# A four-layer conditioned stack: values' products from split operands, the root behind gelu 1, the small network a block later

## The chip, the cores and the metric

One core of one Trainium2 chip. Five engines with queues of their own work beside each other: TensorE (PE; its weight loads are PEld), VectorE (DVE), ScalarE (ACT), GpSimd (POOL) and SyncE (SP), which here issues nearly all DMAs. SBUF is the memory on the chip, PSUM the banks (128 partitions of 512 floats) that TensorE writes. The metric is the device time of one launch in microseconds.

## The reference, cut to what matters

`x` is 64 sequences of 64 tokens of width 256, with one condition vector per sequence. Four layers follow each other: 0, attention with 16 heads of 64, and a gelu MLP of 1024; 1, attention with 16 heads of 16 and a gated MLP of 682; 2, attention with heads of 16, a gelu MLP of 1024 and a gelu-tanh gate (`x + (gelu(v) * tanh(g)) @ W`); 3, a low-rank layer whose matrices a small network makes from the condition. Norms in front of attentions and MLPs are scaled and shifted by the condition. What the change touches:

```python
h = _modulate(_layernorm(x), sh_msa, sc_msa)        # layer 0
q, k, v = jnp.split(h @ W_qkv, 3, axis=-1)          # 16 heads of 64 each
out = jnp.einsum('bhqk,bkhd->bqhd', softmax(q k), v)
y = (x - m) * rsqrt(v + eps)                        
h = gelu(_layernorm(ada_emb) @ W1 + b1); w = h @ W2 + b2   # layer 3's small network
```

## The kernel before, in words

`x` stays in SBUF, transposed (`X`, two halves of 128 features by 4096 tokens), and is worked through in `NCH` = 8 chunks of 512 tokens. The stages follow each other: attention 0, gelu MLP 0 (the first gelu stage), attention 1, gated MLP 1, attention 2, gelu MLP 2 (the second gelu stage), the gelu-tanh gate (the gate stage), the low-rank layer. In each stage an engine has its own hand-written order of instructions and waits on semaphores (`wait_ge`) for what others produce. Between stages stands a barrier.

Where precision must hold and speed too, a float32 operand is split into a high part (float32r, a rounded form) and the remainder; `split3` (L441 to L445) makes three products of float32r operands: low weights by high data, high by low, high by high. `Weights` (L168 to L221) loads raw pieces of 128x512 by groups on SP's queue (`load`), ScalarE copies the high parts (`high`, L196; it waits for a whole group's DMAs), VectorE or POOL subtract the low parts (`low`, L206), and `ready` is TensorE's wait for the first n pieces.

**Attention 0** (L495 on). A step is one pair of heads j of 8 in chunk c. TensorE's step: scores `S` of this pair, transposes of the previous pair's weights (`TRA`) and of the output before (`TRB`), projection of the next pair's Q and K (`pe_proj`, 12 products of 512 columns), the previous pair's output `O`, six output products by `WO`, and, in every second step, `pe_v` (L611): the values of the next two pairs of heads for all 512 tokens, into banks 0 and 1, half of the tokens each. Before, these are float32 products of `H32` and `WV`, 64 tokens as weights by 128 columns, in the two column halves of the array. ScalarE copies bank 0 out (`act_v`, L641), VectorE bank 1 (`dve_v`, L649); the next projection writes over both banks once they are copied. The norm of the next chunk is spread over the steps by constants (`M_NORM` the root and scaling, `M_HH` and `M_HL` the split of H, `M_D`, `M_SQ` and so on). `M_VAR` is step 1 of the next chunk, called tail, where TensorE makes the variance into bank `TRB` and VectorE reads it (`dve_v` of `Front`, L369).

**The start.** SP loads x chunk 0, half of the modulation weights, weight group 0 (four 256 KB pieces of WQK), the other half, chunk 1, `WV` (1 MB), group 1, chunk 2, and later the rest. ScalarE and VectorE split pieces between the first norms.

**Gelu stage** (`feed_forward`, n_m = 8 blocks of 128 hidden features a chunk). TensorE runs the up products three blocks ahead of the down products into four banks. ScalarE writes gelu twice from each bank (`Gf` and the high part `Gh`), VectorE the low part (L1205), then the down products of the block may run. ScalarE waits with gelu m for the split of block m - 2. For the next chunk's norm ScalarE has at block 0 `act_rstd` (L289 to L294: table of ln and exp, the two functions; the gelu table comes back with the next gelu) and VectorE at block 1 Newton's three steps and the scaling (L374 to L382). At a chunk's end VectorE does the variance, the split of the next chunk's block 0 and the residual (L454), POOL adds it to X (L465, `X<-X,RT`).

**Gate stage** (four blocks a chunk; POOL idle). Up products of two matrices (12 products a block) two banks deep, gelu and tanh on ScalarE, on VectorE the product (L1194), high (L1203) and low part (L1205), six down products. Into it the small network of layer 3 is laid (`Hyper`, L1825): ten slots s. TensorE's step of a slot (`tensor`), ScalarE's (`scalar`: copies out or gelu) and VectorE's (`vector`) stood all in the same block: slot 2c in block 1 of chunk c, slot 2c + 1 in block 3, each behind the engine's own work of that block. Slot 0 has a layer norm of the condition in ten small VectorE steps with a root on ScalarE between them.

```python
for m in range(n_m):                      # ScalarE in the gate stage, cut
    act.wait_ge(a_ps.h, a_ps.at(g + 1))   # up products of block m
    nc.scalar.activation(Gf[m % 2][:], src, ACT.Gelu, bias=bias(0, m)).then_inc(g_act.h, 1)
    nc.scalar.activation(Gt[m % 2][:], BK[2 + m % 2][:], ACT.Tanh, bias=bias(1, m)).then_inc(g_act.h, 1)
    hyper.scalar(act, c, m)               # waits for TensorE's step of the slot
```

Of the kernel before, what the change touches and what calls it, by code (L numbers as in the profile page):

```python
# [13 lines left out]
P = 128  # L14
# [10 lines left out]
DH0 = 64  # L25
# [26 lines left out]
def cond_stack_kernel(nc, io):  # L52
    ctx = ExitStack()
    with ctx:
# [61 lines left out]
        c_set, c_sil, c_ang, c_sin, wv_in = count("c_set"), count("c_sil"), count("c_ang"), count("c_sin"), count("wv_in")  # L116
# [119 lines left out]
        class Front:  # L236
# [134 lines left out]
            def dve_norm(self, dve, c):  # L371

# [5 lines left out]
                nc.vector.scalar_tensor_tensor(out=V1[:], in0=V1[:], scalar=1.5, in1=V2[:], op0=ALU.add, op1=ALU.mult).then_inc(f_n3.h, 1)  # L378
                dve.wait_ge(f_n3.h, self.at(f_n3, c + 1))
# [100 lines left out]
        def attention0_plan():  # L480
# [4 lines left out]
            st.WV = place("WV0", [P, DH, 2, PAIRS, DH0], R + 49152)  # L485
# [4 lines left out]
                       for n in ns for k in range(DH)] for ns in ((0, 2), (1, 3))]  # L490
            groups += [[(wo[:, 2 * g:2 * g + 2], WO[0][:, 2 * g:2 * g + 2], WO[1][:, 2 * g:2 * g + 2], WOf[:, 2 * g:2 * g + 2]) for g in range(4)]]
            st.weights = Weights(groups, by_dve=range(8))
            return st

        def attention0(st, nxt):  # L495
            if True:
# [8 lines left out]
                work = Region(R + 57344, END)  # L505
# [105 lines left out]
                def pe_v(pe, G, jj, c, p):  # L611

                    for hf in range(2):
# [20 lines left out]

                def act_v(act, jj, c):
                    if jj % 2 == 0:
# [4 lines left out]
                        nc.scalar.activation(VP[(jj // 2) % 2][:, 0:4], BK[0][:].rearrange("p (b r d) -> p b r d", b=4, r=2), ACT.Copy).then_inc(va_sb.h, 1)  # L641

                def dve_v(dve, jj, c):
                    if jj % 2 == 0:
# [4 lines left out]
                        nc.vector.tensor_copy(VP[(jj // 2) % 2][:, 4:8], BK[1][:].rearrange("p (b r d) -> p b r d", b=4, r=2)).then_inc(vd_sb.h, 1)  # L649


                M_NORM, M_HH, M_HL = 2, 4, 5
# [17 lines left out]
                with nc.Block() as block:  # L670
                    @block.sync
                    def _(sp):
# [5 lines left out]
                        sp.dma_start(WV[:], io["l0_wv"].rearrange("(k p) (a r d) -> p k a r d", p=P, a=2, r=PAIRS)).then_inc(wv_in.h, 16)  # L678
# [14 lines left out]
                    def _(pe):  # L693
# [20 lines left out]
                        pe.wait_ge(wv_in.h, wv_in.at(16))  # L714
# [6 lines left out]
                        def step(c, j, p, more, tail=False, first=False):  # L721
# [65 lines left out]
                            if (not tail and (more or j < PAIRS - 1)) or (tail and more):  # L787
                                if jn % 2 == 0:
                                    pe_v(pe, g + 1, jn, cn, pn)
                            if not first and j == M_MEAN:  # L790
# [11 lines left out]
                        st.weights.ready(pe, st.weights.all())  # L802
# [72 lines left out]
                    def _(dve):  # L875
# [47 lines left out]
                        def step(c, j, p, more, tail=False, first=False):  # L923
# [29 lines left out]
                            if ahead:  # L953
                                dve_v(dve, jn, cn)
# [870 lines left out]
        class Hyper:  # L1825
# [112 lines left out]
            def vector(self, dve, c, m):  # L1938
                s = self.slot(c, m)
                if s is None:  # L1940
                    return
# [257 lines left out]
```

## Time and profile before

| | us |
|---|---|
| median of 3 runs | 2127.19 (2124.84 to 2128.36) |
| the profiled execution | 2128.56 |
| its span, first to last instruction | 2126.8 |
| TensorE busy | 1911.8 |
| VectorE, ScalarE, POOL busy | 1319.5, 994.4, 787.6 |
| mean granted clock of TensorE | 0.96 |

A row of a group of instructions reads: line, engine, operation, output<-inputs, count | busy us, mean ns of one | idle before it and the releaser. A row in order of time: start, length (of the merged run of instructions), engine, line, operation; in brackets what the engine idled before it and for whom. The granted clock is a share of 2.4 GHz: 1.00, or 0.50 for 1.2 GHz. The length of a TensorE record holds its way through the array; how close products follow each other is told by their starts.

### The profile page before, as it was taken

To read this page: it belongs to the slowest core of one execution; us is meant where nothing else is said; L and a number is where in the kernel's file an instruction comes from. 1 tells how busy PE (TensorE), PEld (TensorE's weight loads), DVE (VectorE), ACT (ScalarE), POOL (GpSimd) and SP (SyncE) were. 2 spreads that over 40 slices of the span, in tenths; PEclk is the share of its full clock that TensorE was granted. 3 is DMA by queue.
4 is the path that set the end of the run, shared out by engine and by line. 5 is a ranking of instruction groups with operands and counts; after the bars stand their busy time and mean duration, and the time that the engine had idled before them with its cause. 6 is when DMAs were issued, how large, how long until landed. Compare 5 with 4: busy or idle time off the path is not lost. (4 is left out here: it accounts for less than half of the span.)

```text
span 2126.8 us, 44677 instructions
## 1 busy us (share of the span) xinstructions
PE 1911.8 (90%) x17318; PEld 1485.0 (70%) x17318; DVE 1319.5 (62%) x2028; ACT 994.4 (47%) x1693; POOL 787.6 (37%) x737
## 2 busy tenths in 40 slices
PE   5999999999979998688988899969999799988898
PEld 4777777777867776466766777747777677766675
DVE  4454555555554555588898577768888555544455
ACT  3433433443336666365666344324555466643222
POOL 1220211121123334566677333456878533340000
PEclk8999999999999999799999999979999899999999
DMA  5100000000010000100000000010000000003222
GB/s 184 70 2 2 2 2 2 2 2 2 2 41 21 0 0 1 45 2 3 2 2 2 27 0 0 0 41 2 2 0 2 27 5 0 0 21 103 75 70 80
DMA packets 26300, 44.73 MB, mean 21 GB/s; under 512 B 4240, under 2 KB 12240, under 8 KB 26000
## 3 DMA queue, kind: packets, MB, share of 16 engines
q1 hardware_dynamic: 24848, 42.01, 6.0%
q8 instruction: 132, 2.16, 0.4%
q10 hardware_dynamic: 1280, 0.23, 0.1%
q14 instruction: 40, 0.33, 0.0%
HBM read 35.94 MB, written 6.29 MB: 20 GB/s over the span
## 5 line engine op out<-in xcount | busy, mean ns | idle before, releaser
L1205 DVE TENSOR_TENSOR Glb<-Gfb,Ghb 128x512 fp32r<-128x512 f32 x176 | 165.2, 948 | 97.6 <-ACT Ghb L1156 95.9
L443 PE MATMUL bank<-HH,W1b 128*128 128x512 f32 x448 | 184.9, 413 | 16.1 <-PEq L1511 7.1
L325 POOL TENSOR_TENSOR Tm<-Dv,MOD 128x512 f32<-128x512 f32 x94 | 108.4, 1173 | 236.9 <-DVE Dv L382 159.1
L444 PE MATMUL bank<-HL,W1b 128*128 128x512 f32 x448 | 177.3, 396 | 0.0
L445 PE MATMUL bank<-HH,W1b 128*128 128x512 f32 x448 | 177.2, 396 | 0.0
L443 PE MATMUL O<-Ghb,W2b 128*128 128x512 f32 x352 | 142.9, 406 | 37.1 <-DVE Glb L1205 37.0
L463 POOL TENSOR_TENSOR spare<-RT 128x1 f32<-128x1 f32 x32 | 6.4, 201 | 401.1 <-DVE RT L454 401.1
L314 POOL TENSOR_TENSOR XS<-Tm 128x512 f32<-128x512 f32 x48 | 69.8, 1454 | 219.1 <-ACT Tm L280 214.2
L445 PE MATMUL O<-Ghb,W2b 128*128 128x512 f32 x352 | 138.0, 392 | 0.0
L444 PE MATMUL O<-Glb,W2b 128*128 128x512 f32 x352 | 137.8, 391 | 0.0
L1386 PE MATMUL bank<-WQKa,HH 128*128 128x512 f32 x256 | 91.6, 441 | 38.8 <-DVE HL L390 16.6
L622 PE MATMUL bank<-WV,H 128*64 128x128 f32 x2048 | 120.5, 276 | 2.0 <-ACT Q L631 2.0
L622 PEld LDWEIGHTS bank<-WV,H 128*64 128x64 f32 x2048 | 112.8, 138 | 13.5 <-issue 13.4
L443 PEld LDWEIGHTS bank<-HH,W1b 128*128 128x128 f32 x448 | 85.9, 192 | 41.7 <-issue 17.9
L1662 ACT ACTIVATE PTa<-bank 128x512 f32<-128x512 f32 x128 | 69.2, 593 | 97.6 <-PE bank L1542 97.6
L649 DVE COPY VP<-bank 128x512 f32<-128x512 f32 x32 | 22.1, 691 | 147.9 <-PE bank L622 147.9
L443 PEld LDWEIGHTS O<-Ghb,W2b 128*128 128x128 f32 x352 | 66.3, 188 | 67.9 <-DVE Glb L1205 55.3
L443 PE MATMUL bank<-HH,WQK 128*128 128x512 f32 x256 | 107.5, 420 | 4.3 <-DVE HL L390 4.3
L1155 ACT ACTIVATE Gfb<-bank,bias_cols 128x512 f32<-128x512 f32 x128 | 87.8, 686 | 45.9 <-PE bank L445 37.4
L838 ACT ACTIVATE PT<-bank 128x512 f32<-128x512 f32 x64 | 38.3, 598 | 149.1 <-PE bank L743 148.9
L332 POOL TENSOR_TENSOR H<-Tm,MOD 128x512 f32<-128x512 f32 x94 | 98.5, 1069 | 11.8 <-POOL Tm L325 10.6
L444 PE MATMUL bank<-HL,WQK 128*128 128x512 f32 x256 | 101.6, 397 | 0.0
(262 smaller groups left out, 5161.6 us busy)
## 6 DMA issues: line engine op xcount, KB each, us to landing
w<-l_w_dram SPq DMA_DIRECT2D x33, 256.0 KB, 3.4
X<-xT_dram SPq DMA_DIRECT2D x16, 256.0 KB, 6.7
out_dram<-XO SPq DMA_DIRECT2D x8, 512.0 KB, 2.7
wm<-w_mods_dram SPq DMA_DIRECT2D x4, 768.0 KB, 5.1
W2b_f<-l_w_dram SPq DMA_DIRECT2D x11, 256.0 KB, 5.5
WQK_f<-l_wqk_dram SPq DMA_DIRECT2D x8, 256.0 KB, 8.6
W1b_0f<-l_w_dram SPq DMA_DIRECT2D x8, 256.0 KB, 3.7
wm<-w_mods_dram SPq DMA_DIRECT2D x4, 384.0 KB, 6.3
```

What stands on the lines that cost most here:

```text
L314: nc.gpsimd.tensor_tensor(XS[:], Tm[:, 0], Tm[:, 1], ALU.add).then_inc(f_ss.h, 1)
L325: nc.gpsimd.tensor_tensor(Tm[:, k].rearrange("p (b t) -> p b t", t=T), Dv[:, k].rearrange("p (b t) -> p b t", t=T), m, ALU.mult).then_inc( ...
L332: last = nc.gpsimd.tensor_tensor(H32[p][:, k].rearrange("p (b t) -> p b t", t=T), Tm[:, k].rearrange("p (b t) -> p b t", t=T), m, ALU.add)
L443: nc.tensor.matmul(out, w_lo_ap, x_hi, start=first, stop=False)
L444: nc.tensor.matmul(out, w_hi_ap, x_lo, start=False, stop=False)
L445: return nc.tensor.matmul(out, w_hi_ap, x_hi, start=False, stop=last)
L622: last = nc.tensor.matmul(BK[hf][h2 * T:(h2 + 1) * T, b * P:(b + 1) * P], H32[p][:, k, bb * T:(bb + 1) * T], WV[:, k, h2, jj:jj + 2, :], s ...
L838: nc.scalar.activation(PT[(j + 1) % 2][:].rearrange("p t q -> p (t q)"), TRA[:], ACT.Copy).then_inc(pt_sb.h, 1)
L1155: nc.scalar.activation(Gf[m % 2][:], src, ACT.Gelu, bias=bias(0, m))
L1205: nc.vector.tensor_tensor(Gl[m % gb][:], gf, Gh[m % gb][:].bitcast(F32), ALU.subtract).then_inc(g_lo.h, 1)
L1386: last = nc.tensor.matmul(QKB[:], (HH, HL)[xp][p][:, k, t * P:(t + 1) * P], WQK[wp][:, k], start=(i == 0 and k == 0), stop=(i == 2 and k = ...
L1662: nc.scalar.activation(PT[:, 4 * i:4 * i + 4].rearrange("p r q -> p (r q)"), bank[:], ACT.Copy).then_inc(pt_sb.h, 1)
```

## The change

In attention 0 the values are made from the split H (`HH`, `HL`) and a split `WV`: for each half of the tokens two blocks of 128 tokens, two halves of the features and three products of 256 columns (both heads groups side by side), 24 a call. Since the values now lie 128 tokens deep, each copy to `VP` becomes four of 64 partitions by 256. `WV` is split like the other weights, in pieces 4 to 7 of group 0, loaded with it; `WO` is split a step later, and TensorE waits for it at its first use. `M_HL` moves from 5 to 6; variance and its reader go ahead of the values' work in the tail step. In the gelu stages ScalarE's root moves from block 0 to block 1. In the gate stage TensorE's slots move to blocks 2 and 0 (of the next chunk), ScalarE's and VectorE's parts to blocks 3 and 2; the layer norm and its root stay in block 1 of chunk 0.

```diff
@@ class Front @@
             def dve_norm(self, dve, c):
+                self.dve_newton(dve, c)
+                self.dve_scale(dve, c)
...
@@ attention0_plan @@
-            st.WV = place("WV0", [P, DH, 2, PAIRS, DH0], R + 49152)
+            WV = st.WV = [place(f"WV0_{i}", [P, DH, 2, PAIRS * DH0], R + 49152 + 8192 * i, F32R) for i in range(2)]
+            WVf = place("WV0_f", [P, DH, 2, PAIRS * DH0], R + 49152 + 8192)
+            wv = io["l0_wv"].rearrange("(k p) (a n) -> k p a n", p=P, a=2)
...
+            groups[0] += [(wv[k][:, a], WV[0][:, k, a], WV[1][:, k, a], WVf[:, k, a]) for k in range(DH) for a in range(2)]
...
-            st.weights = Weights(groups, by_dve=range(8))
+            st.weights = Weights(groups, by_dve=range(12))
@@ attention0, pe_v @@
-                        for b in range(CB // 2):
+                        for i in range(2):
+                            tok_ = slice((2 * hf + i) * P, (2 * hf + i + 1) * P)
+                            out = BK[hf][:, i * 2 * P:(i + 1) * 2 * P].rearrange("p (a n) -> p a n", a=2)
                             for k in range(DH):
-                                for h2 in range(2):
-                                    bb = hf * CB // 2 + b
-                                    last = nc.tensor.matmul(BK[hf][h2 * T:(h2 + 1) * T, b * P:(b + 1) * P],
-                                                            H32[p][:, k, bb * T:(bb + 1) * T], WV[:, k, h2, jj:jj + 2, :],
-                                                            start=(k == 0), stop=(k == DH - 1), skip_group_check=True)
+                                for xp, wp in ((0, 1), (1, 0), (0, 0)):
+                                    last = nc.tensor.matmul(out, (HH, HL)[xp][p][:, k, tok_], WV[wp][:, k, :, jj * DH0:(jj + 2) * DH0],
+                                                            start=(k == 0 and wp == 1), stop=(k == DH - 1 and xp == 0 and wp == 0))
                         last.then_inc(v_ps.h, 1)
@@ act_v (dve_v alike, with tensor_copy and the second bank) @@
-                        nc.scalar.activation(VP[(jj // 2) % 2][:, 0:4], BK[0][:].rearrange("p (b r d) -> p b r d", b=4, r=2), ACT.Copy).then_inc(va_sb.h, 1)
+                        for a, b in ((0, 0), (1, 0), (0, 1), (1, 1)):
+                            last = nc.scalar.activation(v_dst(jj, 0, a, b), v_src(0, a, b), ACT.Copy)
+                        last.then_inc(va_sb.h, 1)
...
-                M_NORM, M_HH, M_HL = 2, 4, 5
+                M_NORM, M_HH, M_HL = 2, 4, 6
@@ sync @@
-                        sp.dma_start(WV[:], io["l0_wv"].rearrange("(k p) (a r d) -> p k a r d", p=P, a=2, r=PAIRS)).then_inc(wv_in.h, 16)
@@ tensor @@
-                        pe.wait_ge(wv_in.h, wv_in.at(16))
+                        st.weights.ready(pe, 8)
                         pe_v(pe, 0, 0, 0, 0)
...
                                 if jo == 0:
+                                    st.weights.ready(pe, st.weights.all())
                                     pe.wait_ge(out_taken.h, out_taken.at(2 * c))
...
                             if (not tail and (more or j < PAIRS - 1)) or (tail and more):
+                                if tail and j == M_VAR:
+                                    f, cc = early(fr, nf, c - 1, more)
+                                    f.pe_var(pe, cc)
                                 if jn % 2 == 0:
                                     pe_v(pe, g + 1, jn, cn, pn)
...
-                            if tail and j == M_VAR:
-                                f, cc = early(fr, nf, c - 1, more)
-                                f.pe_var(pe, cc)
...
-                        st.weights.ready(pe, st.weights.all())
@@ scalar @@
                         step(0, 1, 0, 2, first=True)
+                        st.weights.high(act, 4)
@@ vector @@
+                            if tail and j == M_VAR:
+                                f, cc = early(fr, nf, c - 1, more)
+                                f.dve_v(dve, cc)
                             if ahead:
                                 dve_v(dve, jn, cn)
...
-                            if tail and j == M_VAR:
-                                f, cc = early(fr, nf, c - 1, more)
-                                f.dve_v(dve, cc)
...
+                        st.weights.low(dve, 4)
                         step(0, 1, 0, 2, first=True)
@@ feed_forward @@
-                M_NORM, M_HH, M_HL = (1, 4, 4) if n_m == 8 else (1, 3, 3)
+                M_RSTD, M_NEWTON, M_NORM, M_HH, M_HL = (1, 1, 1, 4, 4) if n_m == 8 else (0, 1, 1, 3, 3)
...
-                                if f and f.norm and m == 0:
+                                if f and f.norm and m == M_RSTD:
                                     f.act_rstd(act, cc)
...
+                                if f and f.norm and m == M_NEWTON:
+                                    f.dve_newton(dve, cc)
                                 if f and f.norm and m == M_NORM:
-                                    f.dve_norm(dve, cc)
+                                    f.dve_scale(dve, cc)
@@ class Hyper @@
-                s = 2 * c + {1: 0, 3: 1}.get(m, -99)
+                s = 2 * c + {2: 0, 0: -1}.get(m, -99)
+                return s if s >= 0 else None
+
+            def after(self, c, m):
+
+                s = 2 * c + {3: 0, 2: -1}.get(m, -99)
                 return s if s >= 0 else None
...
             def scalar(self, act, c, m):
-                s = self.slot(c, m)
+                if (c, m) == (0, 1):
+                    act.wait_ge(l3_ln.h, l3_ln.at(6))
+                    nc.scalar.activation(self.st[:, 3:4], self.st[:, 2:3], ACT.Sqrt).then_inc(l3_act.h, 1)
+                s = self.after(c, m)

```

## Rows read from the trace of the kernel before

**Rows 1.** The page of the kernel before: busy time of each engine.
```profile
PE 1911.8 (90%) x17318; PEld 1485.0 (70%) x17318; DVE 1319.5 (62%) x2028; ACT 994.4 (47%) x1693; POOL 787.6 (37%) x737
```

**Rows 2.** Stretches: a chunk, the gate stage. Length; busy PE, PEld, DVE, ACT, POOL; clock; DMA.
```profile
83.60:153.90 70.30, 69.08 (x981) 55.96 (x981) 37.57 (x62) 28.85 (x51) 11.88 (x11) 1.00 0.01 2
...
1907.60:2088.90 181.30, 162.68 (x666) 121.76 (x666) 83.79 (x140) 52.28 (x81) 0.00 (x0) 0.93 0.25 78
```

**Rows 3.** TensorE's waits in the gate stage, then in the first gelu stage.
```profile
PE O L443 <- DVE Glc L1205: 18.5, 6, 4.9
...
PE O L443 <- DVE Glb L1205: 18.2, 19, 1.8
```

**Rows 4.** TensorE in order of time (start us, us): a values' call, the next.
```profile
190.32 3.71 PE L622 MATMUL bank<-WV,H 128*64 128x128 f32 x64
193.96 0.69 PE L734 MATMUL S<-KT,Q 64*64 64x64 f32 x32
```

**Rows 5.** TensorE in order of time: wide split products; a later attention's output products.
```profile
196.21 0.39 PE L443 MATMUL bank<-HH,WQK 128*128 128x512 f32 x1
196.44 0.40 PE L444 MATMUL bank<-HL,WQK 128*128 128x512 f32 x1
...
1500.70 1.16 PE L1577 MATMUL O<-OSa,WOa 128*128 128x128 f32 x8
```

**Rows 6.** Copies and their nearest row (groups, one line's view); engines behind a call.
```profile
L649 DVE COPY VP<-bank 128x512 f32<-128x512 f32 x32 | 22.1, 691 | 147.9 <-PE bank L622 147.9
...
L1430 DVE TENSOR_TENSOR VBa<-bank,VBIa x64: 405/422/429, 1405.1 to 1670.5; 64x256 f32<-64x256 f32 x64
...
197.02 0.64 DVE L942 TENSOR_TENSOR OL<-bank,OH 128x512 fp32r<-128x512 f32 x1
...
198.98 0.50 PE L443 MATMUL O<-OH,WO 128*128 128x512 f32 x1
```

**Rows 7.** The start: one stretch as in rows 2, then engines in order.
```profile
8.20:20.20 12.00, 6.18 (x28) 4.11 (x28) 5.86 (x17) 3.13 (x4) 1.26 (x1) 1.00 0.90 301
...
20.25 2.17 ACT L196 ACTIVATE WQK<-WQK_f 128x512 fp32r<-128x512 f32 x4
...
40.21 3.09 DVE L206 TENSOR_TENSOR WQK<-WQK_f,WQK 128x512 fp32r<-128x512 f32 x4 [3.77 <-ACT WQK L196]
...
42.29 5.38 PE L622 MATMUL bank<-WV,H 128*64 128x128 f32 x64 [2.04 <-ACT Q L631]
```

**Rows 8.** A gelu stage, VectorE, POOL and TensorE in order of time.
```profile
723.63 0.68 DVE L1205 TENSOR_TENSOR Glb<-Gfb,Ghb 128x512 fp32r<-128x512 f32 x1
...
726.25 2.39 POOL L465 TENSOR_TENSOR X<-X,RT 128x1024 f32 x1
...
727.66 1.53 DVE L1205 TENSOR_TENSOR Glb<-Gfb,Ghb 128x512 fp32r<-128x512 f32 x1 [1.63 <-ACT Ghb L1156]
...
729.24 0.50 PE L443 MATMUL O<-Ghb,W2b 128*128 128x512 f32 x1 [0.79 <-DVE Glb L1205]
...
733.16 0.50 PE L443 MATMUL O<-Ghb,W2b 128*128 128x512 f32 x1 [0.91 <-DVE Glb L1205]
```

**Rows 9.** The gate stage: engines in order of time, then stretches as in rows 2.
```profile
1921.28 0.20 ACT L1923 ACTIVATE st<-st 64x1 f32<-64x1 f32 x1 [2.60 <-DVE st L1956]
...
1924.82 1.28 ACT L1158 ACT_TABLE_LOAD   x1
...
1948.95 1.94 PE L1905 MATMUL S<-w,hT 128*64 128x512 f32 x8
...
1954.65 0.79 PE L443 MATMUL O<-Ghc,W2c 128*128 128x512 f32 x1 [3.77 <-DVE Glc L1205]
...
1954.60:1957.40 2.80, 2.75 (x7) 2.17 (x8) 1.72 (x3) 0.00 (x0) 0.00 (x0) 0.50 0.21 80
2052.50:2068.80 16.30, 16.30 (x74) 13.49 (x73) 9.60 (x15) 6.00 (x10) 0.00 (x0) 1.00 0.16 57
1977.60:2004.00 26.40, 23.21 (x97) 16.27 (x96) 11.79 (x19) 8.93 (x15) 0.00 (x0) 0.94 0.25 80
```

More of the change, by code:

```diff
@@ L115, in cond_stack_kernel @@
         x_in = [count(f"x_in{i}") for i in range(3)]
-        c_set, c_sil, c_ang, c_sin, wv_in = count("c_set"), count("c_sil"), count("c_ang"), count("c_sin"), count("wv_in")
+        c_set, c_sil, c_ang, c_sin = count("c_set"), count("c_sil"), count("c_ang"), count("c_sin")
         pos_in, h_lead, ct_in = count("pos_in"), count("h_lead"), count("ct_in")
@@ L371, in dve_norm, with dve_newton @@
             def dve_norm(self, dve, c):
+                self.dve_newton(dve, c)
+                self.dve_scale(dve, c)
+            def dve_newton(self, dve, c):
                 dve.wait_ge(f_rs.h, self.at(f_rs, c + 1))
@@ L504, in attention0 @@
                 nf.live_in(TRB[:], TRB[:], lambda f, pe, c: None, lambda f, pe, c: None, lambda e, c: h_free(e, c + NCH), False, x_final)
-                work = Region(R + 57344, END)
+                work = Region(R + 65536, END)
                 Q = [work.take(f"Q0_{i}", [P, CH]) for i in range(2)]
@@ L633, in act_proj, with v_src, v_dst @@
                     nc.scalar.activation(KT[jj % 2][:], BK[1][:], ACT.Copy).then_inc(ka_sb.h, 1)
+                def v_src(hf, a, b):
+                    return BK[hf][b * T:(b + 1) * T, :].rearrange("p (i a n) -> p i a n", i=2, a=2)[:, :, a]
+                def v_dst(jj, hf, a, b):
+                    return VP[(jj // 2) % 2][a * T:(a + 1) * T].rearrange("p (f i b) r d -> p f i b (r d)", f=2, i=2)[:, hf, :, b]
                 def act_v(act, jj, c):
@@ L648, in dve_v @@
                             dve.wait_ge(o_ps.h, o_ps.at(2 * gr - 2))
-                        nc.vector.tensor_copy(VP[(jj // 2) % 2][:, 4:8], BK[1][:].rearrange("p (b r d) -> p b r d", b=4, r=2)).then_inc(vd_sb.h, 1)
-                M_NORM, M_HH, M_HL = 2, 4, 5
+                        for a, b in ((0, 0), (1, 0), (0, 1), (1, 1)):
+                            last = nc.vector.tensor_copy(v_dst(jj, 1, a, b), v_src(1, a, b))
+                        last.then_inc(vd_sb.h, 1)
+                M_NORM, M_HH, M_HL = 2, 4, 6
                 M_XH, M_MEAN, M_D, M_SQ, M_SQH = 3, 4, 5, 5, 6
@@ L787, in step @@
                             if (not tail and (more or j < PAIRS - 1)) or (tail and more):
+                                if tail and j == M_VAR:
+                                    f, cc = early(fr, nf, c - 1, more)
+                                    f.pe_var(pe, cc)
                                 if jn % 2 == 0:
                                     pe_v(pe, g + 1, jn, cn, pn)
+                            elif tail and j == M_VAR:
+                                f, cc = early(fr, nf, c - 1, more)
+                                f.pe_var(pe, cc)
                             if not first and j == M_MEAN:
@@ L952, in step @@
                                                         ALU.mult).then_inc(o_sb.h, 1)
+                            if tail and j == M_VAR:
+                                f, cc = early(fr, nf, c - 1, more)
+                                f.dve_v(dve, cc)
                             if ahead:
@@ L1938, in vector @@
             def vector(self, dve, c, m):
-                s = self.slot(c, m)
-                if s is None:
-                    return
                 st, ada, ada2, gB = self.st, self.ada, self.ada2, self.gB
-                if s == 0:
+                if (c, m) == (0, 1):
                     dve.wait_ge(l3_in.h, l3_in.at(112))
@@ L1961, in vector @@
                     step(nc.vector.tensor_copy(st[:, 5:6], st[:, 4:5]))
+                s = self.after(c, m)
+                if s is None:
+                    return
                 if s >= 3 and s - 3 < 4:
```

3 lines of the change are left out of this document (1 added, 2 removed).

## The prediction, made before the change was run

> **What bounds the kernel now.** The page comes first: TensorE is busy 90% of the span and no other engine passes 62%, so time is won by taking work off TensorE or by ending its waits [rows 1]. Then the busy time of two stretches [rows 2]. In a steady chunk of the first attention TensorE is busy 69.08 of 70.30 us at the full clock: there its own work is the time, eight such chunks long. The gate stage is busy 162.68 of 181.30 us at a mean clock of 0.93. Last the waits of TensorE: in the gate stage 18.5 us in six waits, all for a split on VectorE; in the first gelu stage 18.2 us in 19 waits for the same line, two in each of its 8 chunks and three more at its end [rows 3]; the second has two in each of 7 chunks. So each part of the change is judged against TensorE: the products directly, the two moved steps by those waits.
>
> **1. The values' products.** Before, one call (a pair of heads' pairs, 32 in all) issues 32 products that show as 64 records: it starts at 190.32 and the next work at 193.96, 3.64 us [rows 4]. After, it issues 24 products of 256 columns against 128 weights. No row shows a product of that kind and width. From above: the same kind with 512 columns starts every 0.228 us (196.21, 196.44, and so on through the 12 of a projection [rows 5]). 24 of those would be 5.47 us, slower than before; that end is the rival below. From below: 512 columns at 2.4 GHz are 0.213 us, so 256 can't go under 0.107, 2.57 us a call. The nearest row in weights and stream is the output product of the later attentions: eight records, each loading 128 weights, take 1.16 us with the last one's 0.275 in it, so 0.126 apart [rows 5]. The 512-column product lies 0.015 over its columns; 0.107 + 0.015 = 0.122 agrees. I take 0.122: 2.93 us a call, 0.71 saved, times 32 = 22.7 us. With 0.112 it would be 30, with 0.133 still 14.
> The loading of weights needs a word. The Trainium skill (TensorE: Matmul & The Clock Gate, Part 3, The mechanism) says that a weight load overlaps a running matmul only where their row groups differ. By that rule every new product, which uses all rows, would pay its load on top, some 0.107 us by the page's weight-load formula: 0.21 each, 5.1 us a call, 47 us lost over the calls. The trace speaks against it: the eight records above have 0.126 between them for load and stream together.
>
> Evictions. VectorE's copy of 128x512 (0.691 us) becomes four of 64x256; the nearest row, 64x256 from PSUM, is 0.422 [rows 6]. Four are 1.7 us, 1 us more per call, and I take the same for ScalarE. ScalarE does its half while TensorE still works on the second. VectorE begins at the call's end; behind its copy it has the maximum, the subtraction, the sum and OL, which starts at 197.02 for a TensorE product at 198.98 [rows 6]: finished 1.3 us early, 0.3 to 0.4 early after the change. Covered, narrowly; were it not, each tenth late costs 3 us over 32 calls. HL moves from a step with a call to one without, and has the time of the products and the next scores. The variance products go ahead of the call in the tail step, and their reader on VectorE ahead of its copies, so the longer copies don't delay the transposes that reuse that bank. Cost zero.
>
> The start. The 1 MB of values' weights is now in the first group, ahead of the second half of the modulation weights and of chunk 1, on SP's one queue. ScalarE's first `high` waits for the whole group, at 20.25. Then 0.5 + 0.8 + 2.1 MB must have landed; the queues moved 301 GB/s from 8.2 to 20.2, 3.6 MB [rows 7]. Just in time. The half behind it (0.8 MB, 2.6 us more at that rate) can be half a microsecond late for TensorE, which later waits for HL anyway. The first call will wait for VectorE's four `low`, 40.21 + 3.09 = 43.3, where it now starts at 42.29 [rows 7]: 1 us. The split of WO is now a step later: four copies on ScalarE, then four on POOL, each pass no shorter than VectorE's 3.09, and the first output products come a step on, some 9 us. 0 to 1 us. I book 1 us in all: **-22 us** for the stage.
>
> **2. The gelu stages.** Now ScalarE does the root (table, logarithm, exponential, table back) ahead of gelu 1; after, behind it. Follow one chunk [rows 8]. Gelu 1 comes behind the root and the load of its table, its split starts at 727.66 and lasts 1.53 us, and TensorE starts at 729.24 after a wait of 0.79. Then VectorE does Newton's three steps, the scaling and the split of block 2, and TensorE goes on at 733.16 after 0.91. After the change gelu 1 is done before the root, its split follows the residual (which ends as POOL begins, 726.2), and the first wait is gone. The second need not be. The split of 1.53 us shows why: VectorE, reading two operands of SBUF, stood still until POOL's X+RT (726.25 to 728.64) ended; by itself such a split is 0.68 (723.63) [rows 8]. Newton's first step, now at about 726.6, gets in ahead of X+RT or waits for it; the second waits in any case until near 729.4 and ends at 730.1. Third step 0.7 (a split's length), scaling 1.2 (twice as wide), split 0.7: TensorE starts block 2 at 732.7 to 733.0 where it was 733.16. The removed wait comes back at the next block. I take 0.35 us for each of the 15 chunks with both waits (8 and 7): **-5 us** (0 to 7; were POOL no obstacle, all of 2 us a chunk, 28 us).
>
> **3. The gate stage.** ScalarE, in block 1 and in block 3, waits for the small network's step that TensorE does behind its own block; only then come the next gelu and tanh and VectorE's three steps. In block 3 two blocks of up products cover that; in block 1 nothing does: the network's step starts at 1948.95 and takes 1.94; then ScalarE copies and does gelu and tanh, VectorE its three steps, and TensorE goes on at 1954.65, 3.77 us idle [rows 9]. After, TensorE's steps stand in blocks 2 and 0, their readers in blocks 3 and 2. The reader in block 3 comes when gelu and tanh of that block are long done, and the next two up products and a down product (4.1 us at least) lie before the first result that it delays; the reader in block 2 finds the step done and has two down products and a up product for cover. Of the 18.5 us in six waits the first has 4.9, one at the stage's end 0.6 (it stays); the other four go, 13.0 in all. The first shrinks: the root of the layer norm stays in block 1, but the copy behind TensorE's transpose no longer sits ahead of the table back. That load stands at 1924.82; behind the root (1921.28, 0.20) it could stand at 1921.5 [rows 9], so TensorE goes on 3.3 us earlier and 1.6 to 1.9 us remain. After such a wait the clock is at 1.2 GHz: 2.80 us at 0.50 [rows 9], in which six products take 2.73 us and not 1.36. Four of these go, 5.6 us, and half of the first one's 2. Sum 13.0 + 3.3 + 5.6 + 1.0, and 0.7 for the pipeline's refill: 23.6. Check: a chunk with the network takes 26.4 us, one without 16.3 at full clock [rows 9]; two steps of 1.94 with their transposes explain about 4.8, so 5.3 a chunk is loss, 21 over four, plus the first one's 4. **-24 us** (-17 to -27). Past SP nothing moves; its weight loads and the writes of the network's results come half a block or more later, and the results are wanted only in the stage that follows, 30 us on.
>
> **Sum.** 22 + 24 + 5 = 51 us off the profiled execution's 2128.56: 2077.6. It stands 1.4 above the median 2127.19, so the forecast for the median is 2076.5.
>
> **The rivals.** (a) The narrow product costs what the wide one does, 0.228: each call takes 5.47 us, 1.83 more than now, +58 over 32 calls; with the -29 of the rest, 2157, slower. It decides from 0.152 a product upward in the stage, from 0.19 in the kernel. For it: no row shows this kind under 512 columns. Against: the 0.126 of rows 5. 5%. (b) The network's waits only change place: some reader or a bank of the pair holds TensorE up in another block. Half of part 3 stays, 2089. For it, ScalarE still waits at each step; against, the cover counted above. 10%. (c) VectorE's four copies come late: with 0.3 to 0.6 us late at 32 calls, 10 to 19 us return, 2087 to 2096. 9%. (d) POOL is in Newton's way less than I say: another 20 us, 2056. Against: the 1.53. 6%. (e) That the change does nothing: excluded by the count, 1024 products become 768 of another kind; the question is their price.
>
> **How the numbers follow.** My case has 70%, with 2062 (0.112 a product, 27 and 7 for the others) to 2098 (0.133, 17 and 0). The range 2060 to 2099 also takes in (b) and (c); outside lie (a), (d) and some of my own spread, under 2 in 10. A measurement tells 0.2%, 4 us, from no change. Faster 0.93, same 0.02, slower 0.05.
>
> **What would show it.** In the profile after: a call of 24 products 2.8 to 3.1 us long and chunks of 67.4 us; no wait of TensorE over 0.4 us behind the four copies; in the gelu stages one wait a chunk, of about 1.5 us, and Newton's second step stretched to over 2 us beside X+RT; in the gate stage one wait near 1.8 us, chunks of 21 us, and a clock at 1.00 from the second chunk on. I am wrong if the call is above 3.4 us, if gate chunks stay above 24 us, or if a gelu chunk is under 25.3 us (now 26.3).

## The result, and the profile after

The changed kernel takes 2075.15 us (median of 4 runs, 2071.4 to 2077.6), the kernel before 2127.65 in runs beside it (2124.8 to 2128.4): ratio 0.975, with an interval of 0.974 to 0.977. The forecast was 2076.5 in a range of 2060 to 2099. The profiled execution has a span of 2073.4 us where the one before had 2126.8, so 53.4 us went; the forecast's sum was 51.

Stage by stage, from TensorE's records. A stage is counted from the end of the last product of the stage before (the first one from the span's start) to the end of its own last product:

| stage | before | after | gone | forecast |
|---|---|---|---|---|
| first attention | 632.3 | 613.3 | 19.0 | 22 |
| first gelu stage | 222.9 | 217.6 | 5.3 | } 5 |
| second gelu stage | 210.6 | 205.8 | 4.8 | } |
| gate stage | 185.7 | 161.6 | 24.1 | 24 |
| all others | 875.4 | 875.1 | 0.3 | 0 |

The page of the changed kernel: TensorE's line, against [rows 1], and the groups of the values' products and VectorE's copies, against [rows 4, 6].
```profile
PE 1872.6 (90%) x16038; PEld 1464.3 (71%) x16038; DVE 1380.5 (67%) x2128; ACT 1028.9 (50%) x1793; POOL 799.0 (39%) x737
...
L669 DVE COPY VP<-bank 64x256 f32<-64x256 f32 x128 | 54.0, 422 | 114.0 <-PE bank L632 112.7
...
L632 PE MATMUL bank<-WV,HH 128*128 128x256 f32 x512 | 98.7, 286 | 2.7 <-DVE WV L206 2.7
```
TensorE has 39 us less work and is still busy 90% of the span, so its waits fell too. VectorE has 61 us more: 32 are the copies, 27 are Newton's second step (L380), which has the same 48 instructions as before and takes 62.2 us where it took 35.1. The copy costs the 422 ns that the nearest row said. The 286 ns of a product hold its way through the array; its price is the distance between starts.

A call of 24 products starts at 294.77 and the next work, at 297.74, is 2.97 us later. Its first products, TensorE in order of time:
```profile
294.77 0.28 PE L632 MATMUL bank<-WV,HH 128*128 128x256 f32 x1
294.88 0.28 PE L632 MATMUL bank<-WV,HL 128*128 128x256 f32 x1
295.01 0.41 PE L632 MATMUL bank<-WV,HH 128*128 128x256 f32 x2
295.25 0.28 PE L632 MATMUL bank<-WV,HL 128*128 128x256 f32 x1
```
2.97 over 24 is 0.124 apiece. Next the stretches (columns as in [rows 2]): two chunks of the first attention, a chunk of the first gelu stage, a gate chunk with the small network and one without.
```profile
291.65:428.38 136.73, 131.61 (x1641) 108.39 (x1640) 84.99 (x147) 65.47 (x124) 23.45 (x21) 1.00 0.01 2
...
727.56:753.39 25.83, 24.33 (x104) 19.07 (x103) 16.18 (x18) 16.38 (x24) 11.16 (x8) 1.00 0.00 0
...
1929.11:1950.39 21.28, 21.28 (x99) 15.11 (x100) 11.97 (x20) 7.22 (x11) 0.00 (x0) 1.00 0.29 99
...
2003.90:2020.20 16.30, 16.30 (x74) 13.49 (x73) 9.60 (x15) 5.99 (x9) 0.00 (x0) 1.00 0.25 85
```
In the gate stage TensorE is busy without a break at the full clock, where the chunk of 26.4 us had 0.94 [rows 9]. The gelu chunk still lacks 1.5 us, the attention's two lack 5.1. The waits that remain say where: the gate stage's two, the gelu stage's, then two groups of the first attention.
```profile
PE O L449 <- DVE Glc L1230: 2.7, 2, 2.2
...
PE O L449 <- DVE Glb L1230: 15.3, 10, 1.8
...
PE O L449 <- DVE OL L966: 7.8, 10, 2.5
PE S L795 <- DVE SP L955: 6.6, 14, 1.3
```
In the gate stage 18.5 us in six waits became 2.7 in two [rows 3]. In the gelu stage 19 waits became 10, but 18.2 us only 15.3: half of the waits went, the others grew. In the first attention TensorE now waits 6.6 us for SP, the scores' subtraction, where the same wait came to 1.8 us before. Behind it stands a second kind of wait (an output product, 3.6 us in six, most of them 0.63) that was not there before. The prediction had ruled out any wait over 0.4 us behind the copies.

### The profile page after: what moved, and what is told of

The parts are those of the page before. It is cut to its first block and busy times, and to the rows that moved or that the text cites. A ratio compares the mean times of both kernels' runs of the same rounds, so it can differ in the third digit from the quotient of the medians.

```text
span 2073.4 us, 42326 instructions
## 1 busy us (share of the span) xinstructions
PE 1872.6 (90%) x16038; PEld 1464.3 (71%) x16038; DVE 1380.5 (67%) x2128; ACT 1028.9 (50%) x1793; POOL 799.0 (39%) x737
## 5 line engine op out<-in xcount | busy, mean ns | idle before, releaser
L1230 DVE TENSOR_TENSOR Glb<-Gfb,Ghb 128x512 fp32r<-128x512 f32 x176 | 155.7, 894 | 67.0 <-ACT Ghb L1181 65.3
L469 POOL TENSOR_TENSOR spare<-RT 128x1 f32<-128x1 f32 x32 | 11.4, 355 | 397.9 <-DVE RT L460 397.9
L669 DVE COPY VP<-bank 64x256 f32<-64x256 f32 x128 | 54.0, 422 | 114.0 <-PE bank L632 112.7
L449 PE MATMUL bank<-HH,WQK 128*128 128x512 f32 x256 | 107.4, 420 | 4.6 <-DVE HL L396 4.6
L451 PE MATMUL bank<-HH,WQK 128*128 128x512 f32 x256 | 101.4, 396 | 0.0
L632 PE MATMUL bank<-WV,HH 128*128 128x256 f32 x512 | 98.7, 286 | 2.7 <-DVE WV L206 2.7
L450 PEld LDWEIGHTS bank<-HL,W1b 128*128 128x128 f32 x448 | 86.0, 192 | 20.8 <-issue 3.3
```

The lines of the kernel that those rows point to most:

```text
L449: nc.tensor.matmul(out, w_lo_ap, x_hi, start=first, stop=False)
L450: nc.tensor.matmul(out, w_hi_ap, x_lo, start=False, stop=False)
L451: return nc.tensor.matmul(out, w_hi_ap, x_hi, start=False, stop=last)
L632: last = nc.tensor.matmul(out, (HH, HL)[xp][p][:, k, tok_], WV[wp][:, k, :, jj * DH0:(jj + 2) * DH0], start=(k == 0 and wp == 1), stop=(k ...
L669: last = nc.vector.tensor_copy(v_dst(jj, 1, a, b), v_src(1, a, b))
L1230: nc.vector.tensor_tensor(Gl[m % gb][:], gf, Gh[m % gb][:].bitcast(F32), ALU.subtract).then_inc(g_lo.h, 1)
```

## The experiments

Ten kernels ran, the last two five times each and the others once. Beside them the kernel before took 2123.4 to 2125.1 us, 2.5 to 4.3 us less than beside the changed kernel, so single times are read only to that accuracy and the stage lengths carry the argument. Their own spread can be read from the stages whose code a run leaves alone. The gelu stages repeat within 0.3 us, with one trace 1.2 us shorter. The gate stage, changed, lies between 160.0 and 162.5 us. The first attention, in the six traces with the changed kernel's code there, lies between 611.4 and 615.6: differences of under 4 us in that stage say nothing.

**One part undone: the gate stage.** The network's step on TensorE and its readers on ScalarE and VectorE go back to blocks 1 and 3.
```diff
- s = 2 * c + {2: 0, 0: -1}.get(m, -99)
+ s = 2 * c + {1: 0, 3: 1}.get(m, -99)
- s = 2 * c + {3: 0, 2: -1}.get(m, -99)
+ s = 2 * c + {1: 0, 3: 1}.get(m, -99)
```


> The changed kernel, with the small network's steps back in blocks 1 and 3 on all three engines. My theory: the gate stage grows by 24 us, from about 157 to 181, with five waits of TensorE of 2.6 to 5 us and stretches at half clock behind them; all other stages stay within 1 us; 2099 us. The rival (the gate stage became shorter through something else, such as the stages ahead of it ending with a warmer clock): it grows by under 15 us.

2099.36 us; the gate stage 187.7 us long, 26 longer than changed. Every wait of before is back, to the tenth [rows 3]:
```profile
PE O L449 <- DVE Glc L1230: 18.5, 6, 4.9
```
So the gate part is worth what the forecast gave it (24.1 by the table above, 26.1 here), and it doesn't depend on the others.

**Another undone: the root in block 0.** `M_RSTD, M_NEWTON, M_NORM, M_HH, M_HL` go from (1, 1, 1, 4, 4) to (0, 1, 1, 4, 4).

> The changed kernel, with ScalarE's root of the gelu stages back in block 0. My theory: a gelu chunk goes from 25.8 back to 26.3 us and has two waits of 0.8 and 0.9 in place of one of 1.5; both gelu stages together lose 7 to 10 us; 2084 us. The rival (the other parts shortened the gelu stages, through the state in which they begin): the two stages stay within 2 us of the changed kernel's.

2089.36 us; the gelu stages 222.8 and 210.5, 5.2 and 4.7 longer. The chunk is 26.3 us again with waits of 0.78 and 0.88. The part is worth 10 us, not 5.

**What holds Newton's step: POOL's pass cut to one token.** In the gelu stages POOL adds RT to X for the first token of a chunk alone; the rest of the residual is left out.
```diff
+ t, r = (bass.ds(c * CH, 1), slice(0, 1)) if one else (tok(c), slice(0, CH))
- nc.gpsimd.tensor_tensor(X[:, :, tok(c)], X[:, :, tok(c)], RT[:], ALU.add)
+ nc.gpsimd.tensor_tensor(X[:, :, t], X[:, :, t], RT[:, :, r], ALU.add)
```


> The changed kernel, but in the gelu stages POOL adds one token of a chunk's residual to X and not all 512 (it leaves out the rest of that sum). My theory, that POOL's long sum keeps VectorE out of Newton's steps: the wait of 1.5 us in block 2 goes nearly whole, a gelu chunk takes 24.2 to 24.6 us, 2075 falls by 18 to 24. The rival, that the wait is VectorE's own chain of split, Newton, scaling and split: the chunk stays above 25.5 us and the time within 5 us.

2042.91 us; gelu stages 204.3 and 194.8, together 24 less than changed. TensorE's row of the first one falls from ten waits to three, all in the last chunk:
```profile
PE O L449 <- DVE Glb L1231: 4.2, 3, 1.5
```
The whole fell by 32, not 24: the gate stage lost 3.8, the second attention 2.5 and the swiglu stage 2.3 as well. A shorter pass at a stage's end may be the reason (see the last run); no run tests that by itself.

The changed kernel shows the same thing from the other side. VectorE and POOL in order of time:
```profile
730.47 0.69 DVE L378 SCALAR_TENSOR_TENSOR V<-V,V 128x512 f32<-128x512 f32 x1
731.19 2.77 DVE L380 TENSOR_TENSOR V<-V,V 128x512 f32<-128x512 f32 x1
734.00 0.69 DVE L382 SCALAR_TENSOR_TENSOR V<-V,V 128x512 f32<-128x512 f32 x1
...
730.56 2.85 POOL L471 TENSOR_TENSOR X<-X,RT 128x1024 f32 x1
```
Newton's second step, 0.69 when left alone, takes 2.77 and ends 0.55 after POOL's pass ends (733.96 against 733.41). The Trainium skill (SBUF — State Buffer, SBUF: two separate sides) says that POOL and a VectorE operation with two inputs in SBUF share one pair of ports by an exclusive lock, and the one that comes second waits for the whole instruction. This trace and this run agree, with 2.77 and 0.69.

**VectorE's residual ahead of its copies.** In the tail step VectorE took the four copies first, then the residual of the chunk before, then the scores' maximum. Now the residual comes first, before the variance's reader.
```diff
 if tail and j == M_VAR:
+    residual(c - 1)
     f, cc = early(fr, nf, c - 1, more)
     f.dve_v(dve, cc)
```


> The changed kernel, but in the first attention VectorE takes the residual of a finished chunk ahead of the variance and of the four copies in step 1, while TensorE makes the values, and not behind them. My theory, that the stage's new waits at a chunk's start (0.47 and 0.63 in step 2) come from copies and residual standing one behind the other: both go, a chunk takes 67.3 to 67.6 us in place of 68.4, the stage is 7 to 9 us shorter, 2067. The rival, that the copies alone (1.7 us) make VectorE late: the waits stay and the chunk is above 68.1.

2065.43 us; the first attention 606.5 us, 6.8 less (7 to 9 were expected). The two later kernels with this order have 606.1 and 605.4, so all three lie at least 4.9 us below the six traces without it. Here is what it cures, in the changed kernel, VectorE and then TensorE in order of time:
```profile
279.69 1.73 DVE L669 COPY VP<-bank 64x256 f32<-64x256 f32 x4 [2.27 <-PE bank L632]
281.45 1.41 DVE L460 SCALAR_TENSOR_TENSOR RT<-O,bias_cols,MOD 128x512 f32<-128x512 f32 x2
282.78 0.68 DVE L952 TENSOR_REDUCE mx<-S 128x8 f32<-128x512 f32 x1
283.49 0.69 DVE L955 TENSOR_TENSOR SP<-S,mx 128x512 f32<-128x512 f32 x1
...
284.44 0.69 PE L795 MATMUL S<-VP,PT 64*64 64x64 f32 x32 [0.47 <-DVE SP L955]
285.76 0.49 PE L449 MATMUL O<-OH,WO 128*128 128x512 f32 x1 [0.63 <-issue]
```
VectorE stood idle 2.27 us ahead of the copies, waiting for the call. The residual fits in there. Behind the copies it makes SP late, and then OL (284.93 to 285.57; the profile names no releaser for the second wait, but OL ends 0.19 us ahead of that product): 0.47 and 0.63 us of TensorE. The pair stands in five of the seven steps of this kind, 5.2 us together; in two, right behind the loop's pause (see below), it is missing. With the order changed all five pairs are gone, and a steady chunk takes 66.8 us (426.28 to 493.06) where it took 68.0. A pair of 1.25 and 0.63 early in the first chunk stays: it has another cause, told under the start.

**Newton's steps a block later.** (1, 1, 1, 4, 4) becomes (1, 2, 2, 4, 4), so that they miss POOL's pass.

> The changed kernel, but in the gelu stages VectorE does Newton's steps and the scaling behind the split of block 2 and not ahead of it; POOL's sum is whole. The same instructions in another order. My theory: split 2 has to wait for POOL's X+RT once (to about 0.5 us behind its end) and is then there before TensorE wants block 2, so the wait of 1.5 us goes; scaling ends at the same time as now, so H comes no later, but TensorE comes 1.7 us earlier to the next chunk's first up product, which wants HL, and 0.5 to 1 us of it may be lost there. A chunk of 24.2 to 25.2 us, 10 to 24 us off the total, 2052 to 2066. The rival, that Newton's steps are on a chain of their own through POOL and HL that sets the chunk: it stays at 25.6 us or more.

2085.49 us; the gelu stages 221.8 and 210.7, 4.2 and 4.9 longer. My expectation missed and the other one held. The wait moved from block 2 to block 4, VectorE and TensorE in order of time:
```profile
694.83 1.22 DVE L364 TENSOR_TENSOR Dv<-X,S 128x1024 f32<-128x1024 f32 x1 [4.52 <-POOL H L332]
695.97 0.69 DVE L1230 TENSOR_TENSOR Glb<-Gfb,Ghb 128x512 fp32r<-128x512 f32 x1
...
696.71 0.50 PE L449 MATMUL O<-Ghb,W2b 128*128 128x512 f32 x1 [1.50 <-DVE Glb L1230]
```
The centring (L364) waits for POOL's H, and the split that TensorE wants stands behind it. A steady chunk is 25.9 us, no better, and the last chunks have longer waits, up to 3.9 us. From the start of POOL's pass, the scaling now starts 5.04 us later where it was 4.16, and H ends 11.15 us later where it was 10.73, while TensorE, without the wait in block 2, comes 1.5 us sooner to block 4. Of the two ways tried in this stage, taking POOL's pass away wins and going round it does not.

**Products of half the width.** Each product of 256 columns is made as two of 128, so a call has 48.
```diff
+for a in range(2):
...
-last = nc.tensor.matmul(out, (HH, HL)[xp][p][:, k, tok_], WV[wp][:, k, :, jj * DH0:(jj + 2) * DH0],
+last = nc.tensor.matmul(out[:, a], (HH, HL)[xp][p][:, k, tok_], WV[wp][:, k, a, jj * DH0:(jj + 2) * DH0],
```


> The changed kernel, but each values' product of 256 columns is made as two of 128 columns, with the same weights loaded for both: 48 products a call, the same columns in sum. What sets the price of a product? If the columns alone do, with 0.015 us over them, a product takes 0.068, the call 3.3 us, and the first attention grows by 10 us. If the load of 128 weights does (0.107 to 0.126 in the nearest rows), it is 0.11 to 0.13, the call 5.2 to 6 us, and the stage grows by 70 to 100 us. If this kind of product costs four times as much under 256 columns, 0.22 a product, the call is 10.6 us and the stage grows by 240 us. I expect the second.

2167.65 us, the first attention 92 longer. Three products take 0.336 us, TensorE in order of time:
```profile
300.00 0.28 PE L633 MATMUL bank<-WV,HL 128*128 128x128 f32 x1
300.11 0.39 PE L633 MATMUL bank<-WV,HH 128*128 128x128 f32 x2
300.33 0.27 PE L633 MATMUL bank<-WV,HL 128*128 128x128 f32 x1
```
So 0.112 us for half of the columns, where 256 columns take 0.124: a product of this kind has a floor of about 0.11 us. 48 by 0.112 is 5.4 us a call, 2.4 more than changed, 77 of the 92 us over 32 calls. Of the other 15, 4.6 are idle time where the loop goes round: four pauses, 8.8 us in all, where the changed kernel has two of 4.2. Over the 7.4 and 7.2 us from the first pause of each pair on, the granted clock is 0.54, which loses 5 us more than in the changed kernel; the rest isn't followed. As expected, the second case held. This run shows a floor, not its cause. That it is the load of a product's 128 weights, which every product has whatever its width, is the likeliest reading; no run tests it.

**HL left where it was.** `M_HL` back from 6 to 5, a step with a call.

> The changed kernel, with the split of H (HL) back in step 5 of the first attention, a step with a values' call, right behind VectorE's four copies. My theory: the copies end 1 us later than before, HL (1.2 to 1.6 us) pushes maximum, subtraction and OL out, and TensorE waits 0.7 to 1.3 us once a chunk before the output product or OL: the stage grows by 5 to 10 us. The rival, that HL is covered in both places: within 2 us.

2090.48 us; the first attention 14.2 us longer, above the 5 to 10 that I expected; the rival (within 2 us) fell. The wait for SP grows from 6.6 us in 14 times to:
```profile
PE S L795 <- DVE SP L955: 14.4, 23, 1.2
...
252.26 1.73 DVE L669 COPY VP<-bank 64x256 f32<-64x256 f32 x4 [3.82 <-PE bank L632]
254.02 1.88 DVE L396 TENSOR_TENSOR HL<-H,HH 128x1024 fp32r<-128x1024 f32 x1
```
There VectorE has HL behind the four copies, in the same step. SP then keeps TensorE waiting 1.06 us in each chunk, and OL, right behind, 0.58 us (the waits for OL grow from 7.8 us in ten to 12.9 in 19). With that order the narrow products would have won 5 us, not 19. The move of HL is what pays out the products.

**POOL's pass a chunk later.** POOL stood idle from 747.66 to 755.87 in the changed kernel's chunk. Its X+RT of a chunk goes there, near the end of the next chunk, in the gelu and swiglu stages.
```diff
-residual_pool(pool, c)
+if c > 0:
+    residual_pool(pool, c - 1)
+if not more:
+    residual_pool(pool, c)
...
-chunks(pool, body)
+chunks(pool, body, True)
```


> The changed kernel with one step of POOL moved: in the gelu and swiglu stages the sum X+RT of a chunk is no longer done right behind the chunk's residual, beside Newton's steps, but near the end of the next chunk, where POOL stood idle from 747.7 to 755.9 and VectorE has nothing but splits. The whole computation is done. Theory (POOL's pass holds VectorE's Newton step, and that is all of the wait of 1.5 us): as with the pass cut to one token, the wait goes and the gelu stages lose 20 to 26 us together, chunk 24.2 us, kernel 2049 to 2055 us. Rival 1 (the gain of the small pass came because POOL had less work in all, or because X was written with less traffic): the gelu stages stay within 5 us of the changed kernel's 217.6 and 205.8. Rival 2 (the pass now holds the splits of blocks 6 and 7 and the wait only changes place): a new wait of TensorE of 0.5 to 1 us a chunk for a split, 8 to 12 us gained.

2058.67 us, 4 above the 2049 to 2055 expected; gelu stages 204.7 and 195.6, together 23 less, as expected. One stretch and the rows of VectorE and POOL show the chunk without a wait, and Newton's step at its own length:
```profile
700.37:724.41 24.04, 24.04 (x104) 19.16 (x103) 15.91 (x19) 17.57 (x24) 10.88 (x8) 1.00 0.00 0
...
704.00 0.69 DVE L380 TENSOR_TENSOR V<-V,V 128x512 f32<-128x512 f32 x1
...
719.11 2.52 DVE L1230 TENSOR_TENSOR Glb<-Gfb,Ghb 128x512 fp32r<-128x512 f32 x1 [0.43 <-ACT Ghb L1181]
...
718.68 2.40 POOL L471 TENSOR_TENSOR X<-X,RT 128x1024 f32<-128x1024 f32 x1
```
The pass now holds a split instead (2.52 us and not 0.68), but that one is early, and TensorE doesn't notice. Some is given back: the second attention takes 2.7 us more and the swiglu stage 4.0. In the last chunk the pass stood behind the fills of the next stage's buffers, and VectorE's last residual waited for it:
```profile
825.36 1.41 DVE L460 SCALAR_TENSOR_TENSOR RT<-O,bias_cols,MOD 128x512 f32<-128x512 f32 x2 [5.77 <-POOL X L471]
```

**Both orders together.** The last one and the residual ahead of the copies.

> Both orders that the runs point to: POOL's X+RT of the gelu and swiglu stages a chunk later, and in the first attention VectorE's residual ahead of the variance's reader and of the four copies of the tail step. The whole computation is done. They touch different stages, so the gains should add: 20 to 26 us in the gelu stages and 6.8 us in the first attention (as measured alone), 2042 to 2049 us against 2075.2 of the changed kernel and 2127.7 of the one before: ratio to the latter 0.960 to 0.963. If the gelu part gives nothing, 2068, ratio 0.972.

2050.55 us median of 5 (2046.8 to 2052.8), ratio to the kernel before 0.965, interval 0.964 to 0.967; slower than the 2042 to 2049 expected, which had left out what the later pass gives back. First attention 606.1 (7.2 less than changed), gelu stages 203.5 and 195.6 (24.3 less), second attention 5.0 more, swiglu 2.0 more.

**The pass ahead of the fills.**

> As the kernel with both orders, but in a stage's last chunk POOL's X+RT of the chunk before comes ahead of the fills of the next stage's buffers and not behind them. In the kernel with both orders it stood behind 8 us of fills, VectorE's last residual waited 5.8 us for it and the second attention began with 9.6 us without a product where the changed kernel had 5.5. Theory: these 4 us come back at the second attention, and up to 2 at the swiglu stage's end: 2044 to 2047 us against 2050.6, ratio to the kernel before 0.962 to 0.964. Rival (the stage waits for the fills themselves, now 2.5 us later): nothing is gained, 2050 to 2053.

2048.45 us median of 5 (2044.5 to 2052.5), ratio 0.965, interval 0.963 to 0.966: not to be told apart from the last. The median lies between what I expected (2044 to 2047) and the rival (2050 to 2053). TensorE's gap at the second attention's start is 8.6 us, 1 less than the 9.6 of the last two kernels and well over the changed kernel's 5.5; the stage takes 317.7 us, where the two kernels with the same later pass took 318.7 and 321.0. POOL and ScalarE at that point, first in this kernel:
```profile
806.54 2.03 POOL L1349 MEMSET VBa<- 128x544 f32 x4
...
814.66 2.34 POOL L471 TENSOR_TENSOR X<-X,RT 128x1024 f32<-128x1024 f32 x1
...
817.32 1.28 ACT L1664 ACT_TABLE_LOAD   x1 [12.25 <-PEq L1112]
```
and in the changed one:
```profile
825.33 2.02 POOL L1345 MEMSET VBa<- 128x544 f32 x4
...
833.50 2.34 POOL L471 TENSOR_TENSOR X<-X,RT 128x1024 f32<-128x1024 f32 x1
...
836.16 1.28 ACT L1660 ACT_TABLE_LOAD   x1 [8.87 <-PEq L1111]
```
In both the next stage begins 0.3 us after POOL's last pass ends. POOL's fills and passes are what the stage's end waits for, and a pass put among them lengthens it, ahead of the fills or behind them. Of the 4 us that were to come back, the gap shows 1, so the rival is the nearer of the two.

## Why the prediction was right

**The price of a product** was the disputed number: 0.122 us taken, 0.124 measured, so 0.67 us a call and 21.4 over 32 calls instead of 22.7. Of the rivals, (a) put it at 0.228 and fell. The other rule it weighed, that the weights' load comes on top (0.21), fell as well: 0.124 and, at half the width, 0.112, both of products that use all rows. Some luck is in how well it fits. The forecast added 0.015 us to the time of the columns; at 128 columns that would be 0.068, and the run of half width has 0.112. And the row of 0.126 that seemed to agree is of float32 products, two records each; float32r products of that width stand 0.112 apart.

**The copies, "Covered, narrowly"**, at a cost of zero, are the step that failed. It counted the copies, the maximum, the subtraction, the sum and OL behind a call, and left out that in the tail step the residual's 1.41 us stand in that queue too. There the slack was used up, and TensorE waited up to 0.47 and 0.63 us where the forecast had "no wait of TensorE over 0.4 us": 5.2 us in five steps. Moving the residual alone gave 6.8 us back, so rival (c) was real, at 5 to 7 us and five calls, not 10 to 19 at 32.

**The move of HL** was also booked at nothing. Its sign is right and its size hidden: left where it was, HL would have cost 14.2 us.

**The start** was booked at 1 us and cost 3.7. Two places make it up. The first is the load that was to be "just in time": ScalarE's first `high` stood ready and waited 0.86 us for the values' weights, and it starts at 21.68 where it was 20.25 [rows 7]. The first call starts 2.5 us later than before (44.77), having also waited 2.7 us and not 2.0 for the last `low` part. When the second scores start, at 63.09 and not 61.86, the start has cost 1.8 us: these 1.2, and 0.8 that the first call had won, less 0.3 by which the first product was later already. The second is WO's split, moved a step later. ScalarE, POOL, VectorE and TensorE of the changed kernel in order of time:
```profile
21.68 2.19 ACT L196 ACTIVATE WQK<-WQK_f 128x512 fp32r<-128x512 f32 x4 [0.86 <-DMA WV_f<-l_wv_dram]
...
71.75 5.01 POOL L206 TENSOR_TENSOR WO<-WO_f,WO 128x512 fp32r<-128x512 f32 x4 [29.38 <-ACT WO L196]
...
73.66 1.95 DVE L583 TENSOR_SCALAR MOD<-MOD 128x128 f32<-128x128 f32 x2
...
77.30 0.69 PE L795 MATMUL S<-VP,PT 64*64 64x64 f32 x32 [1.25 <-DVE SP L955]
```
Beside POOL's passes the two small VectorE steps of L583 take 1.95 us where they took 0.36 before (L574, at 72.25), and TensorE waits 1.25 and then 0.63 us. That POOL's passes hold them is read from the trace; no run moved them.

**What is left open in the attention.** 21.4 less 5.2, less 3.7, less 0.8 for longer waits in the last chunk is 11.7. Two gains are known: TensorE's pauses where the loop goes round (no releaser named) are 2.23 and 1.97 us, together 1.0 less than the 2.74 and 2.50 before, and six small waits for OL of 0.18 us are gone, 1.1. That makes 13.8; the stage lost 19.0. The other 5 us stay open, hardly more than the stage's spread. The term of 22 thus came out near 19 partly by luck. The clock is not what fills the gap. It fell to its lower level behind both pauses before and behind one of two after, first the kernel before, then the changed one:
```profile
214.31:218.00 3.69, 3.69 (x43) 3.38 (x44) 2.18 (x4) 1.23 (x3) 3.14 (x2) 0.50 0.02 4
360.09:364.00 3.91, 3.91 (x44) 3.55 (x45) 2.52 (x5) 1.57 (x3) 3.39 (x2) 0.56 0.02 4
```
```profile
210.96:214.50 3.54, 3.37 (x44) 3.04 (x45) 3.38 (x7) 1.71 (x3) 2.23 (x2) 0.69 0.02 5
349.34:353.00 3.66, 3.50 (x49) 3.11 (x50) 3.47 (x8) 1.82 (x4) 2.09 (x2) 1.00 0.02 4
```
But the changed kernel's clock also fell at 79.20 and 601.40, where the one before had 1.00, and from 60 us to the stage's end both have a mean of 0.99. Nor did the length of a pause decide. Behind one of 2.33 us the run with the gate part undone kept its clock; behind one of 1.80 us the run with Newton's steps a block later did not:
```profile
212.08:215.78 3.70, 3.70 (x50) 3.25 (x51) 3.54 (x7) 2.18 (x4) 2.66 (x3) 1.00 0.01 4
```
```profile
213.28:216.98 3.70, 3.70 (x45) 3.25 (x46) 3.51 (x8) 1.82 (x3) 2.12 (x2) 0.67 0.02 4
```

**The gelu stages** were forecast at 5, in bounds of 0 to 7, and gave 10. The mechanism was right down to its figures: one wait a chunk of 1.50 (about 1.5), Newton's second step at 2.77 (over 2). The term was mis-sized. The chunk fell from 26.3 to 25.83, 0.47 and not 0.35. And it counted every chunk as a steady one. In the first chunk of a stage no pass of POOL stands beside Newton's steps yet, so there both waits went and none came back: 1.7 us in the first stage, 1.4 in the second. With six steady chunks of 0.47 in each that makes 4.5 of 5.3 and 4.2 of 4.8. Rival (d), POOL less in the way, fell: a run without POOL's pass gave 24 us more.

**The gate stage** was right: 24.1, four waits gone, chunks of 21.3 where 21 was said, the clock at 1.00 from the second chunk. The first wait is 2.18 us, and not 1.6 to 1.9. The table's load does stand right behind the root, as the forecast had it; and TensorE goes on 3.3 us earlier after the root's start, as forecast; but it also comes to its stop earlier, 2.65 us after that start where it was 3.21, in part because two transposes (0.33 us) no longer stand ahead of it. A shorter queue ahead of a wait makes the wait longer. Behind this wait the clock still fell (0.53 from 1894.9 to 1898.4), so the 1.0 us booked for it is not seen. Rival (b), the waits change place, fell.

So 51 us were forecast and 53.4 came, with 3 less than forecast in the attention and 5 more in the gelu stages, which partly cancel: the sum is better than its terms.

## What to carry to other kernels

When an engine's work behind an event grows, list its whole queue at every step of the loop, the step with the rare extra work included: the slack must be read at the fullest step, and a piece that can be done ahead of the event belongs there. Here a stall of VectorE beside POOL was cured by moving POOL's pass to where VectorE's operations are early anyway; moving VectorE's own chain only moved the wait, since that chain feeds POOL again. And before filling a gap of an engine at a stage's end, see whether that engine is what the stage's end waits for.

## What the runs showed that I had not expected

- A float32r product with a load of 128 weights of its own takes 0.112 us at 128 columns, 0.124 at 256 and 0.228 at 512. From 512 to 256 nearly half of the price goes, from 256 to 128 a tenth.
- Pauses of TensorE of about 2 us are sometimes followed by a stretch at half clock and sometimes not, in the same code: 2.33 us left the clock at 1.00, 1.80 us was followed by 0.67. A difference of 2 to 4 us in such a stage, from one trace of each kernel, shows no gain.
- One pass of POOL of 2.4 to 2.9 us in each chunk, standing at the wrong place, cost 23 us over two stages.
